# A sphere convolution that measures its own result, and a spectral block that normalises its input

## The reference, cut to what matters

```python
x = x + L0(_gn(x), ...)    # coupled map, small convolutions, gate
x = x + L1(_gn(x), weight, bias)    # sphere convolution
x = x + L2(_gn(x), ...)    # spectral block, four layers
x = x + L3(_gn(x), weight, bias)    # sphere convolution

def _gn(v, G=4, eps=1e-05):
    g = v.reshape(B_, G, C_ // G, H_, W_)
    m = jnp.mean(g, axis=(2, 3, 4), keepdims=True)
    s = jnp.var(g, axis=(2, 3, 4), keepdims=True)
    return ((g - m) / jnp.sqrt(s + eps)).reshape(v.shape)
```

## Time and profile before

| | |
|---|---|
| median of 3 runs | 3428.85 us (3423.66 to 3441.11) |
| the profiled execution | 3424.0 us, span 3422.0 us |
| PE busy | 2749.5 us, 80% of the span |
| DVE busy | 1898.7 us, 55% |
| ACT busy | 1432.5 us, 42% |
| POOL busy | 748.6 us, 22% |
| DMA | 438.03 MB, mean 128 GB/s |
| `sph1` (935 to 1070) | PE busy 111.8 us of 135 |
| `gn2` and the spectral prelude (1070 to 1173) | PE busy 5.1 us of 103 |

### The profile page before, as it was taken

The page is one execution under the profiler, slowest core; times in us unless marked ns, Lnnn a source line. Parts: engine busy times, 40 slices in busy tenths (PEclk is TensorE's granted clock), DMA queues, the critical chain, the costliest instruction groups (busy, mean ns, idle before and its releaser), DMA issues. The chain is left out here.

```text
span 3422.0 us, 44205 instructions
## 1 busy us (share of the span) xinstructions
PE 2749.5 (80%) x17124; PEld 2137.0 (62%) x17124; DVE 1898.7 (55%) x2438; ACT 1432.5 (42%) x2409; POOL 748.6 (22%) x675
## 2 busy tenths in 40 slices
PE   0699996869485299579996899779996699999658
PEld 0244443436253298579895798669985687887535
DVE  6988776735625311245544455355453478878643
ACT  1777775722122122253334333253333466666322
POOL 3988501213110000000000000000000044444310
PEclk9999998989797699789997999889998899999879
DMA  8300006679334566868676676758767634332134
GB/s 206 68 24 0 24 6 164 187 153 203 96 92 132 105 139 143 220 156 203 160 175 202 151 200 160 182 151 190 194 166 185 119 59 85 59 63 49 63 90 95
DMA packets 344001, 438.03 MB, mean 128 GB/s; under 512 B 260422, under 2 KB 302022, under 8 KB 317406
## 3 DMA queue, kind: packets, MB, share of 16 engines
q1 hardware_dynamic: 343319, 430.43, 52.4%
q0 software_dynamic: 496, 5.01, 0.4%
HBM read 258.62 MB, written 168.58 MB: 125 GB/s over the span
## 5 line engine op out<-in xcount | busy, mean ns | idle before, releaser
L1061 DVE STREAM_TRANSPOSE spec_chan<-spec_form_in 128x1024 f32<-128x1024 f32 x256 | 491.7, 1945 | 63.2 <-PE fno_pz L1277 63.2
L1363 ACT ACTIVATE fno_act<-fno_pz 128x320 f32<-128x320 f32 x512 | 223.8, 437 | 616.2 <-PE fno_pz L1277 616.2
L1252 POOL TENSOR_SCALAR fno_minus<-fno_both 96x960 f32<-96x960 f32 x32 | 83.4, 2606 | 1376.7 <-DVE fno_both L1455 1376.7
L1447 DVE COPY fno_wfreq<-fno_pw 128x240 f32<-128x240 f32 x256 | 97.7, 395 | 513.5 <-PE fno_pw L1305 511.5
L1277 PEld LDWEIGHTS fno_pz<-spec_cols,spec_chan 128*128 128x128 f32 x3072 | 348.2, 192 | 12.3 <-issue 9.5
L1277 PE MATMUL fno_pz<-spec_cols,spec_chan 128*128 128x96 f32 x3072 | 350.0, 275 | 2.0 <-ACT spec_cols L1371 2.0
L1328 PE MATMUL fno_pz<-fno_act,fno_wt 128*40 128x64 f32 x2304 | 205.8, 264 | 148.2 <-DMA fno_act<-scratch_modes 107.7
L1581 POOL TENSOR_TENSOR head_hact_lo<-head_hact,head_hact_hi 128x512 fp32r<-128x512 f32 x128 | 227.9, 1783 | 400.7 <-DVE head_hact_hi L1728 400.7
L1305 PE MATMUL fno_pw<-fno_fw,fno_act 128*128 128x96 f32 x2560 | 303.4, 277 | 14.4 <-DVE fno_wfreq L1447 8.6
L1305 PEld LDWEIGHTS fno_pw<-fno_fw,fno_act 128*128 128x128 f32 x2560 | 291.4, 192 | 26.9 <-DVE fno_wfreq L1447 15.4
L1328 PEld LDWEIGHTS fno_pz<-fno_act,fno_wt 128*40 128x40 f32 x2304 | 198.8, 140 | 157.7 <-issue 143.5
(11 more groups left out here) (173 smaller groups left out, 4806.0 us busy)
## 6 DMA issues: line engine op xcount, KB each, us to landing
scratch_form<-fno_act SPq DMA_DIRECT2D x32, 2560.0 KB, 17.2
spec_form_in<-scratch_form SPq DMA_DIRECT2D x64, 1024.0 KB
fno_act<-scratch_modes SPq DMA_DIRECT2D x128, 180.0 KB
nca_raw<-scratch_xnp SPq DMA_DIRECT2D x66, 329.7 KB
fno_coef<-scratch_mixed SPq DMA_DIRECT2D x48, 360.0 KB, 10.9
spec_form_in<-scratch_form SPq DMA_DIRECT2D x32, 512.0 KB
fno_wt<-table_mix_w SPq DMA_DIRECT2D x32, 450.0 KB, 11.1
gn_x<-scratch_x SPq DMA_DIRECT2D x12, 1024.0 KB
```

Of the source, the lines that this page charges most:

```text
L1061: return nc.vector.transpose(chan[:, to * TR * PIX:(to + 1) * TR * PIX].rearrange("p (h q w) -> p h q w", h=TR, q=4), src)
L1363: nc.scalar.activation(act_b[:, n % 2, :, 4 * t:4 * t + 4], z, ACT.Silu if layer else ACT.Copy).then_inc(a_out, 1)
```

## The change

`gn2` and the tensor `xn2` are removed. In `sph1` (not in `sph3`), DVE reduces each output tile over its columns right after it is formed; POOL forms the mean of each row and subtracts it from the tile, ACT squares, and DVE reduces the squares three tiles later (`sum_squares`). At the end PE averages the sums over rows, DVE adds the spread of the row means around the mean to the row squares, PE averages those, and the small chain stores mean and reciprocal root as `stats2`. POOL's centring of window v+2 now stands between the second and the third tile of window v, in both sphere convolutions. The spectral block loads `x2` and DVE normalises each unit in place, on 16 partitions (two operations of 4096 values per partition for a unit), before PE reads it. PE's first product waits for two tables instead of seven; the rest are waited for before the first `forward_cols`. The clearing of `wt` moves behind the first normalisation.

```diff
-def sphere_conv(nc, name, bias, built, stats, xin, xout, nchw=False):
+def sphere_conv(nc, name, bias, built, stats, xin, xout, nchw=False, mask_of=None, out_stats=None):
...
+                        if out_stats is not None:
+                            sp.wait_ge(row_centred, NQ * (v - 1))
...
+                if out_stats is not None:
+                    sp.dma_start(mask[:, :], mask_of).then_inc(mask_in, 16)
+                    sp.wait_ge(ready, 2)
+                    sp.dma_start(out_stats, small[:, 3:5, :]).then_inc(stats_out, 16)
...
+                def centre_rows(n):
+                    v, q = n // NQ, n % NQ
+                    m = sum(b - a for a, b in plan[v][1]) * C
+                    tile = lambda ap: ap.rearrange("p (b w) -> p b w", w=W)
+                    pool.wait_ge(summed, n + 1)
+                    nc.gpsimd.tensor_scalar(row_mean[0:m, n % 2, :], row_sums[0:m, v, BPB * q:BPB * (q + 1)], 1.0 / W, None, ALU.mult).then_inc(averaged, 1)
+                    pool.wait_ge(averaged, n + 1)
+                    if n >= 2:
+                        pool.wait_ge(squared, n - 1)
+                    nc.gpsimd.tensor_tensor(tile(cen[0:m, n % 2, :]), tile(res[0:m, v % 2, q * NB:(q + 1) * NB]), wide(row_mean[0:m, n % 2, :], W, 2), ALU.subtract).then_inc(row_centred, 1)
+
+                centre_window(0)
+                centre_window(1)
+                for v in range(wins):
+                    for q in range(NQ):
+                        if q == 2 and v + 2 < wins:
+                            centre_window(v + 2)
+                        if out_stats is not None:
+                            centre_rows(v * NQ + q)
...
+                def square(n):
+                    m = sum(b - a for a, b in plan[n // NQ][1]) * C
+                    act.wait_ge(row_centred, n + 1)
+                    if n >= 2:
+                        act.wait_ge(sq_summed, n - 1)
+                    nc.scalar.activation(sq[0:m, n % 2, :], cen[0:m, n % 2, :], ACT.Square).then_inc(squared, 1)
+
                 for v in range(wins):
+                    if out_stats is not None and v >= 2:
+                        for n in range((v - 2) * NQ, (v - 1) * NQ):
+                            square(n)
...
+                if out_stats is not None:
+                    for n in range((wins - 2) * NQ, N):
+                        square(n)
...
                         n += 1
+                        if out_stats is not None:
+                            dve.wait_ge(out_ready, n)
+                            if n == 1:
+                                dve.wait_ge(blank, 2)
+                            nc.vector.reduce_sum(row_sums[0:m, v, BPB * q:BPB * (q + 1)], r.rearrange("p (b w) -> p b w", w=W), AX.X).then_inc(summed, 1)
+                            if n >= 3:
+                                sum_squares(n - 3)
...
+                if out_stats is not None:
+                    sum_squares(N - 2)
+                    sum_squares(N - 1)
+                    dve.wait_ge(sq_summed, N)
+                    dve.wait_ge(mean_done, 1)
+                    spread_of_rows(nc, dve, row_sums[:, :, :], row_squares[:, :, :], dev[:, :, :], mean, step, spread_done)
+                    dve.wait_ge(var_done, 1)
+                    reciprocal_root(nc, dve, small, mean, var, step, rooted, ready)
...
+                    pe.wait_ge(mask_in, 16)
+                    pe.wait_ge(summed, N)
+                    row_means(nc, pe, row_sums, mask, mean, rows).then_inc(mean_done, 1)
+                    pe.wait_ge(spread_done, 1)
+                    row_means(nc, pe, row_squares, mask, var, rows).then_inc(var_done, 1)
...
-                                     xn2[:, :, u * 4 * W + t * PIX:u * 4 * W + t * PIX + PIX].rearrange("h c f -> c h f")).then_inc(unit_in[u % 2], 16)
+                                     x2[:, :, u * 4 * W + t * PIX:u * 4 * W + t * PIX + PIX].rearrange("h c f -> c h f")).then_inc(unit_in[u % 2], 16)
...
+                for t in range(S2):
+                    for i in range(2):
+                        sp.dma_start(norm[t * C:t * C + C, i, :, :], stats[0:C, i, :].rearrange("c (u t b) -> c u t b", t=S2, b=B2)[:, :, t, :]).then_inc(norm_in, 16)
+                sp.dma_start(wz[:, :], k["fc0"]).then_inc(first_in, 16)
...
-                pe.wait_ge(set_up, 2)
-                pe.wait_ge(blank, 2)
-                pe.wait_ge(blank_half, 2)
-                pe.wait_ge(tables, 16 * 7)
+                pe.wait_ge(blank, 1)
+                pe.wait_ge(blank_half, 1)
+                pe.wait_ge(first_in, 32)
...
-                            pe.wait_ge(unit_in[u % 2], unit_loads(n))
+                            pe.wait_ge(normed, B2 * (n + 1))
...
                 def forward_cols(n):
                     pe.wait_ge(a_out, (n + 1) * NZ)
+                    if n == 0:
+                        pe.wait_ge(set_up, 2)
+                        pe.wait_ge(blank, 2)
+                        pe.wait_ge(blank_half, 2)
+                        pe.wait_ge(tables, 16 * 5)
...
-                nc.vector.memset(wt[64:128, :, :, :], 0.0).then_inc(wt_blank, 1)
...
                 dve.wait_ge(beta_in, 32)
+                dve.wait_ge(norm_in, 64)
...
+                def normalise(n):
+                    dve.wait_ge(unit_in[n % 2], unit_loads(n))
+                    for b in range(B2):
+                        x = form_in[0:S2 * C, n % 2, :].rearrange("p (h b w) -> p h b w", b=B2, w=W)[:, :, b]
+                        nc.vector.tensor_scalar(x, x, norm[:, 1, n, b:b + 1], norm[:, 0, n, b:b + 1], ALU.subtract, ALU.mult).then_inc(normed, 1)
+
+                normalise(0)
+                nc.vector.memset(wt[64:128, :, :, :], 0.0).then_inc(wt_blank, 1)
                 dve.wait_ge(step, 16)
-                dve.wait_ge(tables, 16 * 7)
+                dve.wait_ge(tables, 16 * 5)
...
                             row_spectra(n - 1)
+                        if not layer and u + 1 < UNITS:
+                            normalise(n + 1)
...
-    group_norm(nc, "gn2", s["x2"], k, dst_plain=s["xn2"])
```

More of the change, by code:

```diff
@@ L393, in _, with row_means, spread_of_rows, reciprocal_root @@
                     nc.vector.tensor_tensor(normed(t), centre(t), wide(small[:, 3, :], W, 2), ALU.mult).then_inc(ready, 1)
+def row_means(nc, pe, part, mask, out, rows):
+    for v, n in enumerate(rows):
+        mm = nc.tensor.matmul(out, mask[0:n, :], part[0:n, v, :], start=v == 0, stop=v == len(rows) - 1)
+    return mm
+def spread_of_rows(nc, dve, row_sums, row_squares, dev, mean, step, spread_done):
+    p, v = row_sums.shape[0], row_sums.shape[1]
+    nc.vector.scalar_tensor_tensor(out=dev, in0=row_sums, scalar=1.0 / W, in1=wide(mean[0:p], v, 1), op0=ALU.mult, op1=ALU.subtract).then_inc(step, 1)
+    dve.wait_ge(step, 1)
+    nc.vector.tensor_tensor(dev, dev, dev, ALU.mult).then_inc(step, 1)
+    dve.wait_ge(step, 2)
+    nc.vector.scalar_tensor_tensor(out=row_squares, in0=dev, scalar=float(W), in1=row_squares, op0=ALU.mult, op1=ALU.add).then_inc(spread_done, 1)
+def reciprocal_root(nc, dve, small, mean, var, step, rooted, ready):
+    nc.vector.tensor_scalar(small[:, 0, :], var, 1e-5, None, ALU.add).then_inc(step, 1)
+    dve.wait_ge(rooted, 1)
+    nc.vector.reciprocal(small[:, 2, :], small[:, 1, :]).then_inc(step, 1)
+    dve.wait_ge(step, 4)
+    nc.vector.tensor_tensor(small[:, 3, :], small[:, 2, :], small[:, 2, :], ALU.mult).then_inc(step, 1)
+    dve.wait_ge(step, 5)
+    nc.vector.tensor_tensor(small[:, 4, :], small[:, 3, :], small[:, 0, :], ALU.mult).then_inc(step, 1)
+    dve.wait_ge(step, 6)
+    nc.vector.tensor_scalar(small[:, 5, :], small[:, 4, :], -0.5, 1.5, ALU.mult, ALU.add).then_inc(step, 1)
+    dve.wait_ge(step, 7)
+    nc.vector.tensor_tensor(small[:, 3, :], small[:, 5, :], small[:, 2, :], ALU.mult).then_inc(ready, 1)
+    nc.vector.tensor_copy(small[:, 4, :], mean).then_inc(ready, 1)
 def coupled_map(nc, k_local, k, xnp, cmp_, sphere):
@@ L908, in sphere_conv @@
             ph.sem(n) for n in ("acc_done", "out_ready", "centred", "scaled", "hi_laid", "lo_laid", "lo_copied", "mats_hi", "mats_split"))
+        N = wins * NQ
+        if out_stats is not None:
+            cen, sq = ph.sb("cen", [104, 2, NB]), ph.sb("sq", [104, 2, NB])
+            row_sums, row_squares, dev = (ph.sb(n, [104, wins, B]) for n in ("row_sums", "row_squares", "dev"))
+            row_mean, averaged = ph.sb("row_mean", [104, 2, BPB]), ph.sem("averaged")
+            mask, small = ph.sb("mask", [128, 128]), ph.sb("small", [128, 6, B])
+            mean, var = acc[:, 4, 0:B], acc[:, 5, 0:B]
+            mask_in, blank, summed, row_centred, squared, sq_summed, mean_done, spread_done, var_done, step, rooted, ready, stats_out = (
+                ph.sem(n) for n in ("mask_in", "blank", "summed", "row_centred", "squared", "sq_summed", "mean_done", "spread_done", "var_done", "step", "rooted", "ready", "stats_out"))
         def loads(v):
@@ L965, in _, with centre_window @@
                 pool.wait_ge(tables, 32)
```

(26 more changed lines are left out.)

16 lines of the change are left out of this document (11 added, 5 removed).

## The result

The changed kernel takes 3392.7 us (median of 5 runs, 3387.0 to 3415.9) against 3428.9 (5 runs, 3418.5 to 3441.1). The ratio is 0.990, with a 95% interval of 0.988 to 0.992. In a second set it was 3392.3 (4 runs) against 3430.1 (8 runs), 0.989 (0.987 to 0.991). Forecast: 3392, 3373 to 3409.

The account below looks back on a forecast made before the run. No engine is full around the change; chains between phase barriers bound it. Saving 19.8 us (parts 1 to 3) plus 13.3 (prelude), 33.1 off 3424.0, gave 3390.9; forecast 3392 us, range 3373 to 3409.

Parts of the forecast that it names:

- Part 1: Norm phase gn2 between first sphere convolution and spectral block: all its 50.5 us go, its work reappearing elsewhere.
- Part 2: First sphere convolution, measuring its result: last output 20 us later, PE stalling some 11 us at windows 3 and 4.
- my walk: Sphere convolution windows 2 to 4 worked through in time order: window 4's copy ends at 1075.5, last output at 1090.
- Part 3: Tail of sph1: mask lands 6.8 us after the last output, spectral block starts 17.5 us after it.
- my two ends: Tail of sph1: spectral block starts 17.5 us after the last output with a late mask, lower end 13.7.
- Part 4: Prelude of the spectral block: PE starts at 32.4 us instead of 45.7, saving 13.3; upper normalisation price saves 9.
- D: Rival, prelude: gains only the moved clearing's 5.8 us, as beta_in comes later behind norm loads; 3400 us, chance 0.10.
- Part 5: Layer 0 of the spectral block: normalise(n+1) in DVE's queue is covered, each of six times, costing nothing.
- A: Rival, sphere convolution: it hides the new work, 18 us more saved, 3374 us; chance 0.13.
- B: Rival, sphere convolution: POOL hand-offs cost 2.5 us a tile; with 4.5 us normalisations 3408 us; chance 0.12.
- C: Rival, layer 0: slower than before, DVE's normalisation waiting for load_x(n+1) holds up PE's column matmuls; 3442 us, chance 0.05.

Follow-up runs that it names:

- own_norm: Changed kernel with the norm's own phase back for the statistics alone, the spectral block still normalising its input: 3401.0 us, ratio 0.992.
- mask_beta: Changed kernel with the mask loaded ahead of window 1's residuals, and betas and w_bias ahead of wz: 3373.5 us (1 run).
- all_tables: Changed kernel with PE again waiting for every table and clearing before its first matmul; moved wt clearing stays: 3392.9 us (1 run).
- scale_early: Changed kernel with POOL centring at the first tile, ACT squaring two tiles after its conversions, DVE scaling between second and third tile: 3386.0 us (1 run).

## Why the prediction was right

The forecast of the time, of the mechanism and of nearly every term held:

| step | predicted | measured |
|---|---|---|
| sphere convolution longer by | 20 | 20.4 (21.3 again) |
| tail | 17.5 | 16.2 |
| mask usable after the last output | 6.8 | 5.97 (1112.12 to 1118.09) |
| prelude | 32.4 | 31.3 |
| `w_bias` after `load_x(0)` issued | 18.5 | 18.1 (1132.84 to 1150.92) |
| two normalising operations | 4.6 | 4.72 |
| stretch shorter by | 33.1 | 35.5 (34.6 again) |

- **Part 1** held: `gn2` is gone with its 50.5 us. own_norm shows how much of that could be had without part 2: all but 9.5 us of the sum.
- **Part 2** held in size and in cause. I had worked through window 3 and put a stall of some 11 us there, ended by ACT; the trace has 7.39 + 2.60, and 6.86 + 1.75 in window 4, where I had about 11 again. That the walk hits so closely is luck in part: counted from the first DMA of the stage, the copy of window 3 ends at 118.25 us in both, and yet several pieces were off and cancelled. The subtraction of 512 elements costs 1.04 us and not 1.3, the small scaling 0.23 and not 0.5, a tile of DVE 1.97 and not 2.13. Against that, a small scaling that starts beside a two-input operation of DVE takes 2.33 to 2.80, and the low part of window 2 came 1.3 us later than in my walk: I had given this hold-up to large POOL operations only. By the Trainium skill ("SBUF — State Buffer", Who interferes with whom) the port pair is locked for a whole instruction; with that the trace agrees, 0.23 against 2.33. The slower matmuls after each stall I hadn't counted at all. They make PE busy for 5.1 us more, most of it in front of a wait that was there anyway. The copy of window 4 ends at 138.8 us, 1.3 earlier than in my walk (1075.5, which is 140.1). From its end (1094.40 + 1.91) to the last output it took 15.8 us, to 1112.12, where I took over 14.5 from the kernel before, so they and what else is in there are some 1.3 us at the end, and the two differences of 1.3 cancel too.
- **Part 3** held: the mask, 64 KB issued right behind the last store, was usable 5.6 us after its issue (1112.49 to 1118.09) and ended last. It was 0.8 us earlier than I let it be, and each of the two groups of matmuls took 2.34 us where I had 2.7. mask_beta shows the price of the late mask, 4.9 us, more than the 3.8 between my two ends (17.5 and 13.7): there the means are ready before the last squares, and DVE goes on 3.6 us after the last output, against 8.4 here. The first group of matmuls, which then comes right behind PE's work, takes 1.27 us instead of 2.34.
- **Part 4** held at its end, for the terms on the path. One of the side estimates failed: I put the other tables at 40 us, from 35 us between `load_x(0)` and `spec_wsm` before. all_tables has them at 34.2. The 35 us were not a property of the table: 4 of them were the weight loads behind it, which the moved clearing also moves, and over 16 pass in each kernel before the table is even issued (1113.05 to 1129.40 in all_tables), 11.0 of them in SP's issues of unit 1's input and of the coordinates (3.90 and 7.07). It had no effect on the forecast, since this wait was covered either way. But the split was wrong: D prices the moved clearing alone at 5.8 us, which leaves 7.5 of the 13.3 to the lifted wait. The clearing alone is worth 11.5 (45.7 - 34.2), and the lifted wait on top of it 2.9 (34.2 - 31.3).
- **Part 5** held. The input of unit 2 is issued at 1176.37 and that of unit 3 at 1203.56; a period of 27.2 us as before (1190.32 to 1217.51), and after its first matmul PE never waits for the normalisation in layer 0: its waits up to 1400 us are the same 4.2 and 0.5 us in both kernels. On POOL `fno_minus` pays for it, 5.97 us where it met it (its mean went from 2606 ns to the 3240 below), with 1344 us of idle time ahead of its 32 executions:

```profile
L1372 POOL TENSOR_SCALAR fno_minus<-fno_both 96x960 f32<-96x960 f32 x32 | 103.7, 3240 | 1344.3 <-DVE fno_both L1587 1344.3
```

Of the rivals, **A** (the new work hides, 18 us more) wasn't what happened, but 70% of it was to be had with another order (12.7 of 18, scale_early). **B** needed a POOL that takes 2.5 us a tile; it took 1.27 except beside a scaling. **C** needed `load_x` to land 24 us or later; in layer 0 the normalisation of unit 2's input begins 15.3 us after the issue (1176.37 to 1191.66). **D** (betas later behind the norm loads) didn't come, they landed 18.1 us after `load_x(0)`; but that they set the prelude was right, and mask_beta made 9.0 us out of it.

What is open: the first profile of the changed kernel reached `gn1` 22.1 us late and was 5.5 us longer in the rest, the second 7.1 late and 0.6 longer. No run was made to find where this spread between executions comes from.

## What to carry to other kernels

A statistic fused into a producer can cost more by its place in the engines' queues than by its engine time; here 12.7 of 20.4 us were the order. Put the added small operations behind the conversion that the matmuls wait for, and look at what runs beside them. When a pass over memory goes away, look at the small loads that were hidden in it: here a mask, and `betas` with `w_bias`, worth 13.7 us together, became the last thing waited for. And loads issued behind a small table can delay it, here by 4 us; when it is the last one waited for, hold those back or put it first.

## What the runs showed of the hardware

- An operation of 8 elements a partition on POOL takes 0.23 us, but 2.21 to 3.40 where a two-input operation of DVE of 2048 elements (2.29 us) starts beside it or up to 0.43 us behind it. Why one that begins behind it still holds it up is open, and was not tried by itself. It works the other way as well: in scale_early DVE's low part took 5.41 instead of 2.29 us beside a centring that had begun 0.36 us earlier.
- The same holds for a one-input operation with its scalars read from memory: the normalisation of 2 x 4096 elements in 4.72 us stretched `fno_minus` to 5.97, and took 5.38 itself.
- The granted clock was 0.51 in the 7 us after a stall of 7.4 us, with PE busy for 4.4 of them and a second wait of 2.6 among them, and 0.54 in the 8 us after the next stall (1092 to 1100), with PE busy for 6.07. It was 1.00 in the stretches behind both (1079 to 1085, 1100 to 1112).
- A load of 512 KB into 16 partitions in two DMAs is usable 13.0 us after its issue, and one of a few KB behind it 18 us after the same moment. By the Trainium skill ("DMA: Bandwidth & Descriptors", Queues, rings and completion order) descriptors on one engine are consumed in ring order; with that agrees that the same small loads, put ahead, no longer ended last. That loads issued behind a table delay it (17.4 and 17.7 us against 13.4 to 13.7) doesn't follow from that order.
